# Eight-layer gated cross-attention model: the fourth layer finishes eight of its sixteen sequences within its steps, the last layer finishes the other eight, and the last routing runs over 4, 4 and 8 sequences

## What is computed

```
def _L3_xattn_ref(q, k, v, mask, gamma, beta):
    logits = where(mask == 0, NEG, q @ k.T / sqrt(256))
    x = softmax(logits) @ v
    xhat = (x - mean(x)) * rsqrt(var(x) + 1e-5)
    return xhat * gamma + beta

def _L3_ffn_ref(x, Wg, bg, Wi, Wo, A, B):           # 4 experts, rank 4, F = 1024
    scores = softmax(x @ Wg.T + bg);  topv, topi = top_k(scores, 2)
    base = x @ Wi.T;  lora = (x @ A[e].T) @ B[e].T   # for each expert e
    h = relu(base + lora);  out = sum over the two chosen e of w_e * (h_e @ Wo.T)

x = x + tanh(g_xattn[3]) * _L3_xattn_ref(_layernorm(x), ctx, ctx, mask, gamma, beta)
x = x + tanh(g_ffn[3])   * _L3_ffn_ref(_layernorm(x), ...)
```

## Time and profile before

| | us |
|---|---|
| median of 3 runs | 1607.42 |
| lowest and highest run | 1606.39, 1613.87 |
| the profiled execution | 1603.92 |
| its span, first to last instruction | 1602.1 |
| PE busy | 1324.1 (83%) |
| DVE busy | 1130.4 (71%) |
| ACT busy | 906.0 (57%) |
| POOL busy | 728.4 (45%) |
| mean granted clock of PE | 0.912 |

### The profile page before, as it was taken

The page is one execution under the profiler, slowest core; times in us unless marked ns, Lnnn a source line. Parts: engine busy times, 40 slices in busy tenths (PEclk is TensorE's granted clock), DMA queues, the critical chain, the costliest instruction groups (busy, mean ns, idle before and its releaser), DMA issues. The chain is left out here.

```text
span 1602.1 us, 28284 instructions
## 1 busy us (share of the span) xinstructions
PE 1324.1 (83%) x9624; PEld 1110.0 (69%) x9642; DVE 1130.4 (71%) x2469; ACT 906.0 (57%) x1952; POOL 728.4 (45%) x753
## 2 busy tenths in 40 slices
PE   2689977899999999869974779899778965555898
PEld 0445555799999999735554779899776842345687
DVE  6447756688988988559966558778565649785654
ACT  3236652677877877457732447777426347464432
POOL 2223202367777777413321038888403930454444
PEclk8699997999999999889995789999899979676899
DMA  5000003456656656320014027676511000101000
GB/s 186 1 1 1 1 14 127 180 221 247 269 219 258 262 216 258 109 63 1 1 56 166 4 91 250 225 242 240 184 39 50 1 0 1 33 1 62 1 27 27
DMA packets 60780, 173.69 MB, mean 108 GB/s; under 512 B 10256, under 2 KB 42000, under 8 KB 51040
## 3 DMA queue, kind: packets, MB, share of 16 engines
q1 hardware_dynamic: 53152, 151.42, 26.4%
q0 software_dynamic: 7488, 20.46, 3.7%
HBM read 155.34 MB, written 16.52 MB: 107 GB/s over the span
## 5 line engine op out<-in xcount | busy, mean ns | idle before, releaser
L1812 POOL TENSOR_TENSOR l0m_e_DL<-l0m_e_DN,l0m_e_DH 128x256 fp32r<-128x256 f32 x192 | 183.4, 965 | 86.6 <-ACT l0m_e_DH L1655 85.5
L1720 DVE TENSOR_TENSOR l0m_e_UL<-l0m_e_U,l0m_e_UH 128x512 fp32r<-128x512 f32 x192 | 164.5, 862 | 10.7 <-ACT l0m_e_UH L1645 10.4
L1581 PE MATMUL PS<-l0m_e_CH,l0m_e_UH 128*128 128x256 f32 x480 | 138.5, 289 | 2.0 <-DVE l0m_e_CL L1755 2.0
L1581 PE MATMUL PS<-l0m_e_CH,l0m_e_UL 128*128 128x256 f32 x480 | 136.5, 284 | 0.0
L1581 PE MATMUL PS<-l0m_e_CL,l0m_e_UH 128*128 128x256 f32 x480 | 136.4, 284 | 0.0
L1645 ACT CAST l0m_e_UH<-l0m_e_U 128x512 fp32r<-128x512 f32 x192 | 118.1, 615 | 0.0
L1720 DVE TENSOR_TENSOR l1m_e_UL<-l1m_e_U,l1m_e_UH 128x512 fp32r<-128x512 f32 x96 | 85.5, 892 | 19.9 <-ACT l1m_e_UH L1645 19.2
L1812 POOL TENSOR_TENSOR l1m_e_DL<-l1m_e_DN,l1m_e_DH 128x256 fp32r<-128x256 f32 x96 | 85.2, 899 | 25.5 <-ACT l1m_e_DH L1655 24.4
L1581 PEld LDWEIGHTS PS<-l0m_e_CH,l0m_e_UH 128*128 128x128 f32 x480 | 92.8, 193 | 2.2 <-ACT l0m_e_UH L1645 2.2
L1581 PEld LDWEIGHTS PS<-l0m_e_CL,l0m_e_UH 128*128 128x128 f32 x480 | 92.9, 194 | 0.0
L1581 PEld LDWEIGHTS PS<-l0m_e_CH,l0m_e_UL 128*128 128x128 f32 x480 | 92.7, 193 | 0.0
(11 more groups left out here) (610 smaller groups left out, 4752.9 us busy)
## 6 DMA issues: line engine op xcount, KB each, us to landing
l0m_e_U<-in_l_up SPq DMA_DIRECT2D x24, 2048.0 KB
l0m_e_DN<-in_l_down SPq DMA_DIRECT2D x24, 1024.0 KB, 5.0
l1m_e_U<-in_l_up SPq DMA_DIRECT2D x24, 1024.0 KB, 6.4
l1m_e_DN<-in_l_down SPq DMA_DIRECT2D x24, 512.0 KB, 3.9
CTX<-in_ctx SPq DMA_DIRECT2D x2, 2048.0 KB, 10.4
l1a_GA<-results_by_choice SPq DMA_DIRECT2D x16, 256.0 KB, 6.0
l1m_c_GA<-results_by_choice SPq DMA_DIRECT2D x16, 256.0 KB, 4.7
Z<-in_l_b_rows SPq DMA_DIRECT2D x24, 128.0 KB
```

The costliest lines, as they stand in the source:

```text
L1581: ins = nc.tensor.matmul(hb(u)[:, a * SLOTS:(a + 1) * SLOTS], w[:, f % RING, k, a, :], x[:, t % 2, k, :], start=(p == 0), stop=(p == len(p ...
L1720: nc.vector.tensor_tensor(UL[:, f % RING, :, :, :], U[:, t % 2, :, :, f * P:(f + 1) * P], UH[:, f % RING, :, :, :].bitcast(F32), ALU.subtr ...
L1812: nc.gpsimd.tensor_tensor(DL[:, f % RING, :], DN[:, t % 2, f, :], DH[:, f % RING, :].bitcast(F32), ALU.subtract).then_inc(s_dl, 1)
```

## The change

**In `l3_attention`**, the tail is gone. Inside the steps DVE now aggregates the statistics of Y at once (`bn_aggr` in `y_stats`) and one step later writes (Y - mean) * gamma into Z (`scaled`). For the first `EARLY` = 8 sequences the inverse square root is computed on DVE by twelve small operations (`inverse_root`: a first guess from the bits, then three Newton rounds), three in each of steps 14 to 17, and in steps 18 to 21 DVE does the addition to X (`add_rows`) and the statistics of X, two sequences in each. POOL's second loop and ACT's square root and sixteen normalisations are removed. The layer ends with sequences 8 to 15 not yet added.

**In `l3_ffn`**, the late eight get the square root of their Y variance (`deviation(3, ...)`), DVE adds them to X between the steps of the first routing, takes their statistics just before the unit loop, computes their inverse root by another twelve small operations in unit steps 1 and 2, ACT normalises them in unit steps 4 to 7, and PE turns them in unit steps 5 to 8. Routing runs over three groups: 0 to 3 as before, 4 to 7 (DVE steps 0 to 4), and 8 to 15 (logits at PE steps 9 and 10, DVE steps 11 to 13, exponential at ACT step 11). Pieces 6 to 11 move from steps 9 to 11 to steps 13 and 14. `HR` gets a buffer of its own, because Z's upper half now holds the late sequences. `LO` is cleared by two smaller memsets that wait for `s_ok`.

```diff
+        def inverse_root(c, k, lo, hi, W, WI):
+            v, y = SMALL[:, 0, lo:hi], RSTD[:, lo:hi]
+            c.wait()
+            if k == 0:
+                c.step(nc.vector.tensor_scalar(WI, v.bitcast(I32), 1, None, ALU.logical_shift_right))
+            elif k == 1:
+                c.step(nc.vector.tensor_scalar(y.bitcast(I32), WI, -1.0, float(0x5f3759df), ALU.mult, ALU.add))
...
@@ l3_attention, DVE @@
                             nc.vector.bn_stats(STATS[:, b, :], Y[:, b, :]).then_inc(s_ys, 1)
+                            dve.wait_ge(s_ys, b + 1)
+                            ch.step(nc.vector.bn_aggr(MV[:, b, :], STATS[:, b, :]))
...
+                            if 6 <= t < B + 6:
+                                scaled(t - 6)
...
+                            if NEWTON < t <= NEWTON + 4:
+                                for k in range(3 * (t - NEWTON - 1), 3 * (t - NEWTON)):
+                                    inverse_root(ch, k, 0, EARLY, NW[:, :], NI[:, :])
+                            if NEWTON + 4 < t <= NEWTON + 8:
...
+                                    add_rows(b)
...
+                                    x_stats(b)
-                        row_scales(ch, s_var, 0, B)
-                        row_factors(dve, ch, s_sd, 3, s_ok, 0, B)
-                        for b in range(B + 3):
-                            if b < B:
-                                dve.wait_ge(s_hat, b + 1)
-                                nc.vector.tensor_tensor(Z[:, b, :], Z[:, b, :], GB[:, 0, :], ALU.mult).then_inc(s_gm, 1)
-                            if b >= 3:
-                                x_stats(b - 3)
@@ l3_ffn @@
-                group = (slice(0, FIRST), slice(FIRST, B))
+                group = (slice(0, FIRST), slice(FIRST, EARLY), slice(EARLY, B))
...
-                first_piece = {6: (3, 5), 7: (5, 6), 9: (6, 8), 10: (8, 10), 11: (10, 12)}
-                SPLIT = FIRST + 4
+                first_piece = {6: (3, 4), 7: (4, 5), 8: (5, 6), 13: (6, 8), 14: (8, 12)}
+                late_turn = {5: 4, 6: 5, 7: 6, 8: 7}
+                late_logits = {9: (EARLY, EARLY + 4), 10: (EARLY + 4, B)}
...
@@ PE @@
-                            if u < 2:
-                                logits(1, SPLIT + u * 4, SPLIT + u * 4 + 4)
+                            if u in late_turn:
+                                turn(late_turn[u])
+                            if u in late_logits:
+                                logits(2, *late_logits[u])
@@ ACT @@
+                            if 4 <= u < 8:
+                                normalise(EARLY + 2 * (u - 4))
+                                normalise(EARLY + 2 * (u - 4) + 1)
+                            if u in late_turn:
+                                columns(late_turn[u])
+                            if u == 11:
+                                exponential(2)
@@ POOL @@
-                            if u in (3, 6, 8):
-                                diagonal({3: 1, 6: 2, 8: 3}[u])
+                            if u in (3, 11, 12):
+                                diagonal({3: 1, 11: 2, 12: 3}[u])
@@ DVE, ahead of the units and in them @@
-                        for i in range(4, pairs):
-                            normalise(2 * i)
-                        columns(2)
+                        for b in range(EARLY + 4, B):
+                            add_rows(b)
                         softmax(0)
...
+                        for b in range(EARLY, B):
+                            x_stats(b)
...
+                            if u == 0:
+                                shifted(1)
...
+                            if u in (1, 2):
+                                for k in range(6 * (u - 1), 6 * u):
+                                    inverse_root(ch, k, EARLY, B, NW[:, :], NI[:, :])
...
                             if u == 3:
-                                softmax(1)
-                                order(1)
+                                choose(1)
                             if u == 4:
-                                choose(1)
-                            if u == 5:
                                 parts(1)
+                            if u == 11:
+                                shifted(2)
+                            if u == 12:
+                                softmax(2)
+                                order(2)
+                                choose(2)
+                            if u == 13:
+                                parts(2)
```

More of the change, by code:

```diff
@@ L3131, in _ @@
                             nc.gpsimd.tensor_tensor(X[:, b, :], X[:, b, :], GB[:, 1, :], ALU.add).then_inc(s_xb, 1)
[L3132 to L3135, removed]
+                        pool.wait_ge(s_xb, B)
                     @block.vector
@@ L3372, in _ @@
                         logits(0, 0, FIRST)
-                        for i in range(2, pairs):
+                        for i in range(2, early):
                             turn(i)
-                        logits(1, FIRST, SPLIT)
-                        pe.wait_ge(s_one, 3)
+                        logits(1, FIRST, EARLY)
+                        pe.wait_ge(s_one, 4)
                         for q in range(3):
@@ L3491, in _ @@
                         nc.gpsimd.memset(SC[:, :, :], -1.0).then_inc(s_one, 1)
[L3492 removed]
                         nc.gpsimd.memset(ONES[:, :], 1.0).then_inc(s_one, 1)
+                        pool.wait_ge(s_ok, 2)
+                        for at in (E4 * RK, 32 + E4 * RK):
+                            nc.gpsimd.memset(LO[:, :, :, at:at + E4 * RK], 0.0).then_inc(s_one, 1)
                         for n, (lo, raw, high) in enumerate(((WIL, WI, WIH), (WOL, WO, WOH))):
@@ L3645, in _ @@
                                 read(u - 2)
+                            if u == 0:
+                                shifted(1)
+                                for b in range(EARLY, B):
+                                    ch.step(nc.vector.bn_aggr(MV[:, b, :], STATS[:, b, :]))
+                                ch.wait()
+                                ch.step(nc.vector.tensor_scalar(SMALL[:, 0, EARLY:B], MV[:, EARLY:B, 1], LN_EPS, None, ALU.add))
+                            if u == 1:
+                                softmax(1)
+                            if u in (1, 2):
+                                for k in range(6 * (u - 1), 6 * u):
+                                    inverse_root(ch, k, EARLY, B, NW[:, :], NI[:, :])
                             if u == 2:
-                                shifted(1)
+                                ch.wait()
+                                nc.vector.scalar_tensor_tensor(out=SMALL[:, 2, EARLY:B], in0=MV[:, EARLY:B, 0], scalar=-1.0,
+                                                               in1=RSTD[:, EARLY:B], op0=ALU.mult, op1=ALU.mult).then_inc(s_ok, 1)
+                                order(1)
                             if u == 3:
-                                softmax(1)
-                                order(1)
+                                choose(1)
                             if u == 4:
-                                choose(1)
-                            if u == 5:
                                 parts(1)
+                            if u == 11:
[6 more added lines that the diff above has]
+                                parts(2)
                             if u >= 4:
```

155 lines of the change are left out of this document (110 added, 45 removed).

## The result

| | before | after |
|---|---|---|
| median of 20 runs each, us | 1605.54 | 1610.28 |
| lowest and highest, us | 1598.60, 1613.87 | 1601.86, 1618.67 |
| span of the profiled execution, us | 1602.1 | 1608.6 |

The ratio of the times is 1.0032, with a 95% interval from 1.0017 to 1.0046: slower by 0.3%, less than the 0.5% that was taken for visible. The profiled executions stand 6.5 us apart, the medians 4.7 us.

The account below looks back on a forecast made before the run. Before 1501 us what PE waits for (mostly DVE) bounds the kernel, after it PE's work. Terms 0.7 - 3.4 - 2.9 + 12.9 = +7.3 us on the median 1607.4 give 1614.7, rounded down to 1614.0; range 1601 to 1622.

Parts of the forecast that it names:

- The case forecast as likeliest: Last layer: PE waits over 5 us at piece 6, and the sum is +4 to +12 us; chance 0.45.
- Term A: Fourth attention: the removed tail was DVE at work, and what DVE gets instead costs about as much; +0.7 us.
- Term B: Last layer up to the first unit: WIL ends 1.9 us sooner, then 1.5 us less to LO; -3.4 us.
- Term C: First unit to the end of `second(9)`: waits and half clock 5.9 us where 9.0 were, work changed too; -2.9 us.
- Term D: From `second(9)` to `down(8)`: PE waits 6.5 us for the late LO, then half clock, second wait, added pieces; +12.9 us.
- The second wait: PE's step 14: piece 11 waits for the diagonal of block 3, behind POOL's unit 12; 2.9 us more.
- Rival 1: DVE's steps 11 to 13: late eight routed under cover, Term D 6.7 us or less, total -3 us; chance 0.20.
- Rival 2: Attention steps stretch and PE's clock stays down, in all terms 16 us slower, 1623; chance 0.13.
- Rival 3: No change: LO about as late as forecast, but half clock and second wait don't show; +3.4 us, 1610.8; chance 0.22.

Follow-up runs that it names:

- b2_covered: The change, with each `scaled` in the fourth attention put between the next sequence's statistics and aggregate; ratio to the kernel before 1.0016 (0.9990 to 1.0042).
- b1_rows_first: a1_banks with `rows(0)` and `hidden_low(9)` ahead of the late group's parts on DVE, and `cols_low(2)` behind them; ratio to the kernel before 0.9955.
- b4_all: b3_rows_adds with the attention order of b2_covered; ratio to the kernel before 0.9945 (0.9917 to 0.9973).
- c1_diag: b1_rows_first plus b2_covered, diagonals of blocks 2 and 3 back behind POOL's units 11 and 12; median 1590.51 us, ratio to the kernel before 0.9903.
- a1_banks: The change, with pieces 6 to 11 in PSUM banks 4 and 5 and in PE's steps 15 to 17; ratio to the kernel before 0.9973 (0.9941 to 1.0004).
- b3_rows_adds: b1_rows_first with units 9, 10 and 11 added by DVE and not POOL; ratio to the kernel before 0.9985 (0.9963 to 1.0006).
- a3_cols_low: The change, with `cols_low(2)` on DVE moved from step 11 to step 14, behind the late group's routing; ratio to the kernel before 1.0049.

## Why the prediction came out right, and where it was right by luck

The forecast was +7.3 us for the profiled execution, rounded down to 1614.0; it was +6.5, and 1610.3 by the median. Between the medians of 20 runs each it is +4.7, and the kernel before stands 1.9 us lower there than in the three runs that the forecast started from. The case forecast as likeliest (PE waits over 5 us at piece 6, sum between 4 and 12) is what happened. Term by term:

- **Term A, +0.7:** +0.3. The tail of the earlier trace rows was DVE's work and its replacement cost as much. The 5.1 us for 16 aggregates were the right price of a poor order: b2_covered gets 4.7 us back with the same instructions. The small operations took 0.16 to 0.17 us and started 0.20 us apart, as priced. The Trainium skill (VectorE: DVE Perf Modes, "The TRN2 errata") gives, besides the 58 cycles that the prediction weighed, about 150 cycles as the fixed term measured on a long copy; that is an estimated 165 ns for 8 elements, and the trace agrees. (The 1612.7 that the prediction has for the 58 cycles should read 1613.0, as 1614.7 less 1.7.)
- **Term B, -3.4:** -3.4. PE's first turn still waited for BM, now 14.0 us, and the root's table load stayed hidden. Against the layer's first aggregate WIL ended 1.8 us sooner (1.9 forecast), and from there to LO it took 1.7 us less (1.5 forecast; the numbers given there make 1.9 before the allowance for loss, not 1.7). So the mechanism was right too.
- **Term C, -2.9:** -6.1. This step failed: "the clock falls behind them (as it fell behind the 2.1 us before), 2.4: 5.9 in all". There was a wait of 1.7 us for `read(1)` and one of 0.3 us for a copy of LT, and the clock stayed up: 2.0 us in place of 5.9. That is 3.9 us, of which 3.2 came out; the other 0.7 is not traced. `read(0)` was where it was forecast, 6.8 us behind the first unit, and `first(4)` could just start. The fall of the clock, taken over from the 2.1 and 3.7 us of the earlier trace rows, does not follow a wait of 1.7 us.
- **Term D, +12.9:** +14.1. LO was done 12.9 us behind the end of `second(9)`, 13.1 were forecast, and PE waited 6.3 us for 6.5. The three operations held by POOL took 0.9, 0.9 and 1.0 us more than alone, priced at 1.1 each. The second wait came in three pieces, 0.2, 1.5 and 0.8, for 2.9. The half clock was the part undersized: behind the first wait it lasted 5.3 us, which costs 2.7 for 1.7, and it had a second spell of 3.3 us behind `down(8)`. That is the +1.6 us of the last stretch, which the prediction held to be the same work in the same time. 0.8 us of the +14.1 are in none of these.

So C was 3.2 us too dear and D with its sequel 2.8 us too cheap. Most of both errors is half clock, put behind the wrong waits (2.4 us too much in C, 2.6 too little in D and behind it); one cancelled the other, and the sum came out better than its parts. Rival 1 (routed under cover) had the right mechanism at the wrong place: DVE's 13 us can't be hidden in front of piece 6, but piece 6 can stand 7 us later, and then it is faster than before: by the ratios in b1_rows_first, b4_all and c1_diag, while those of a1_banks and b3_rows_adds are not clear of 1. Rival 2 fell with its clock in term C. Rival 3 fell too: half clock and the second wait did show. Only the traces say so, since its +3.4 us lies nearer to the +4.7 of the medians than the forecast does.

The Trainium skill (SBUF — State Buffer, "SBUF: two separate sides") says of the ports that DVE and GpSimd (POOL here) share that whichever instruction is first has them whole, and the other is blocked to its end; an operation of DVE wants them when it has two inputs in SBUF, against one of GpSimd that reads SBUF, or when it runs in a mode that uses two ports. The runs agree in both directions: 0.19 us became 1.13 on DVE, and the diagonal's 1.04 became 2.02 on POOL in a3_cols_low. The cast, 0.29 and 1.31 us, has one input; whether it ran in such a mode no run here shows.

## What to carry to other kernels

Ask of a wait which of its two ends can move: here the late data could hardly come sooner, but the instruction that waited for it stood ahead of work that needed only its bank, and moving that gave 8 us. Where each step of an engine issues an operation and then one that waits for it, put an independent one between them, and see that the wait counts only what it needs. Before an operation with two inputs in SBUF is moved on DVE, look up what POOL does at the new place.
